# First pass's chunk steps placed ahead for all chunks, and the last block's first tiles prepared beside the last pairs

## The reference, cut to what matters

```python
xn = _layernorm(x, axis=-1)
x = x + _L0_gnn_ref(xn, ..., edge_index, edge_type_8) + _L0_mix_ref(xn[None], ...)[0]      # attention over edges, 8 heads
x = x + _L0_ffn_ref(_layernorm(x, axis=-1)[None], ...)[0]                                  # shared MLP + 2 of 8 experts
xn = _layernorm(x, axis=-1)
x = x + _L1_gnn_ref(xn, edge_index, ...) + _L1_mix_ref(xn[None], ...)[0]                   # GCN, then GAT
x = x + _L1_ffn_ref(_layernorm(x, axis=-1)[None], ...)[0]                                  # MLP of the better half of the nodes
```

## Time and profile before

| what | us |
|---|---|
| median of 3 runs | 2853.38 (2851.15 to 2854.49) |
| profiled execution | 2854.25 |
| its span | 2852.4 |

### The profile page before, as it was taken

One profiled execution on the slowest core, in us unless ns is written; L12 is line 12 of the kernel. 1 busy time (PEld: TensorE's weight loads), 2 busy tenths in 40 slices (PEclk: granted clock), 3 DMA queues, 4 the chain that ended last, 5 costly groups with the idle time before them and its releaser, 6 DMA issues. The chain is left out here.

```text
span 2852.4 us, 42642 instructions
## 1 busy us (share of the span) xinstructions
PE 2291.0 (80%) x11329; PEld 1711.2 (60%) x11329; DVE 1313.4 (46%) x3497; ACT 1076.8 (38%) x2885; POOL 1377.5 (48%) x1407
## 2 busy tenths in 40 slices
PE   6899847767677988999997787877754888875798
PEld 5455535445455877888886465554543777764577
DVE  6553456766676130111114232242248666655851
ACT  3323544545441211333333443265420665542221
POOL 0122477777730051212211677767767777775300
PEclk9999867888788899999998898888775999998899
DMA  3466544444411025777774433344557444443201
GB/s 98 153 219 220 181 110 122 119 120 118 119 50 41 10 95 152 196 221 205 210 211 130 141 106 106 106 122 124 162 147 236 125 132 134 131 123 116 95 12 33
DMA packets 249527, 374.45 MB, mean 131 GB/s; under 512 B 66472, under 2 KB 186740, under 8 KB 249322
## 3 DMA queue, kind: packets, MB, share of 16 engines
q0 software_dynamic: 70000, 179.80, 22.8%
q1 hardware_dynamic: 132740, 140.88, 16.1%
q10 hardware_dynamic: 46582, 51.38, 5.5%
HBM read 298.68 MB, written 73.27 MB: 130 GB/s over the span
## 5 line engine op out<-in xcount | busy, mean ns | idle before, releaser
L2724 POOL DMA_INDIRECT cm_rows<-rows,e_bsrc x392 | 373.3, 952 | 179.0 <-issue 101.2
L1181 POOL DMA_INDIRECT store<-rows,e_bsrc x392 | 377.3, 963 | 119.5 <-issue 107.3
L1459 POOL DMA_INDIRECT at_rows<-values,e_brow x362 | 344.8, 953 | 115.1 <-issue 90.5
L2861 PE MATMUL cm_part<-cm_rows,cm_one 128*128 x880 | 268.0, 447 | 89.8 <-SPq L2737 62.8
L1539 PE MATMUL at_part<-at_msg,store 128*128 128x265 f32 x880 | 269.1, 448 | 86.8 <-DVE at_msg L1695 42.7
L1206 PE MATMUL banks<-ag_msg,ag_one 128*128 128x258 f32 x880 | 228.0, 397 | 70.3 <-issue 45.7
L2861 PEld LDWEIGHTS cm_part<-cm_rows,cm_one 128*128 128x128 f32 x880 | 181.7, 220 | 158.7 <-issue 134.9
L1539 PEld LDWEIGHTS at_part<-at_msg,store 128*128 128x128 f32 x880 | 175.8, 218 | 156.7 <-DVE at_msg L1695 66.7
L2161 POOL DMA_INDIRECT x_sum<-x_y,x_target x56 | 87.1, 1555 | 340.7 <-DVE x_y L2274 333.3
L3077 DVE TENSOR_TENSOR store<-store,cm_part 128x256 f32 x220 | 92.2, 419 | 339.1 <-PE cm_part L2861 311.1
L1206 PEld LDWEIGHTS banks<-ag_msg,ag_one 128*128 128x128 f32 x880 | 165.4, 195 | 117.2 <-issue 57.3
(11 more groups left out here) (685 smaller groups left out, 3920.2 us busy)
## 6 DMA issues: line engine op xcount, KB each, us to landing
x_w<-in_L_ffn_W1p SPq DMA_DIRECT2D x32, 1024.0 KB, 5.2
x_w<-in_L_ffn_W2p SPq DMA_DIRECT2D x32, 1024.0 KB, 5.5
values<-at_rows ACTq DMA_DIRECT2D x25, 1088.0 KB, 6.0
p_brow<-local_row SPq DMA_DIRECT2D x44, 320.0 KB, 4.0
xn_acc<-low_row SPq DMA_DIRECT2D x28, 448.0 KB
expert_in<-store POOLq DMA_DIRECT2D x7, 1040.0 KB, 8.1
at_rows<-values,e_brow POOLq DMA_INDIRECT x392, 2.8
cm_rows<-rows,e_bsrc POOLq DMA_INDIRECT x392, 2.7
```

What stands on the lines that cost most here:

```text
L1181: pool.indirect_dma_start(rows[:, b % slots, k, :], None, table, bass.IndirectOffsetOnAxis(index[:, k, b:b + 1], 0)).then_inc(gathered[b % ...
L1459: pool.indirect_dma_start(rows[:, b % RING, k, :], None, table, bass.IndirectOffsetOnAxis(e.block_row[:, k, b:b + 1], 0)).then_inc(gathere ...
L2724: pool.indirect_dma_start(rows[:, b % SLOTS, k, :], None, table, bass.IndirectOffsetOnAxis(e.block_src[:, k, b:b + 1], 0)).then_inc(gather ...
L2861: last = pe.matmul(part[:, n % deep, :], one[:, n // U % 2, k, u, :], rows[:, bass.ds(at[u] % SLOTS, 1), k, :].squeeze(1), start=(k == 0), ...
```

## The change

In `attend`, PE's six steps of every chunk after the first stand at the pairs lo − 10, − 7, − 6, − 5, − 4 and − 2, and ACT's slope, exponent and fade at lo − 9, lo − 3 and lo, as they did for the last chunk alone; DVE's steps stay. FREE becomes 25: ACT fetches the scores of 25 pairs ahead and SP frees a block 25 blocks after it. In `convolve_and_mix`, AIMED has 23 as well, so four more tiles are scattered there and two are left for `score2`. In `aggregate`, a new class `FirstTiles` loads the table rows and x rows of tiles 0 to 4 after block 98's arrival, and DVE does the degree operations, join, divide, residual and statistics for these five tiles between pairs 202 and 214. In `finish`, group 0 is no longer fetched or prepared: DVE copies the statistics, goes on with variance, root and slots of group 0, then does the degree operations for all tiles, then `prepare(1)`. The loads are put in another order, and w1 and b1 have a semaphore of their own.

```diff
...
                 sp.sem_inc(ready, 1)
+                if b == NB // 2:
+                    firsts.fetch(sp)
...
+                firsts.work(dve, n, summed)
...
+    def fetch(self, sp):
+        sp.wait_ge(*self.gate)
+        sp.dma_start(self.h, self.table[0:U * P].rearrange("(t p) d -> p t d", p=P)).then_inc(self.loaded, 16)
+        sp.dma_start(self.x, self.x_rows[:, 0:U, :]).then_inc(self.loaded, 16)
...
+    def work(self, dve, n, summed):
+        at = n - (NB + U + 1)
+        if at == 0:
+            dve.wait_ge(summed, NB + U - 1)
+            self.ahead(dve)
+            self.link(dve, dve.tensor_scalar(self.some, self.degree[:, 0:U], 1.0, None, ALU.is_lt))
...
+            dve.wait_ge(self.loaded, 32)
+        if at in range(1, 2 * U + 4):
+            self.ahead(dve)
+        for u in range(U):
+            if at == 2 * u + 1:
+                self.link(dve, dve.scalar_tensor_tensor(out=self.h[:, u, :], in0=self.h[:, u, :], scalar=self.own[:, u:u + 1], in1=self.acc[:, u, 0:D],
+                                                        op0=ALU.mult, op1=ALU.add))
+            if at == 2 * u + 2:
+                self.link(dve, dve.scalar_tensor_tensor(out=self.h[:, u, :], in0=self.h[:, u, :], scalar=self.inv[:, u:u + 1], in1=self.bias[:],
+                                                        op0=ALU.mult, op1=ALU.add))
+            if at == 2 * u + 3:
+                self.link(dve, dve.scalar_tensor_tensor(out=self.x[:, u, :], in0=self.h[:, u, :], scalar=0.0, in1=self.x[:, u, :],
+                                                        op0=ALU.max, op1=ALU.add))
+            if at == 2 * u + 4:
+                self.link(dve, dve.bn_stats(self.st[:, u, :], self.x[:, u, :]))
...
-RING, FREE = 28, CH + LEAD
+RING, FREE = 28, CH + LEAD + 3
...
-    pe_steps, act_steps = ({n: step for n, step in step_of.items() if step[1] != last_at} for _ in range(2))
-    pe_steps.update({last_at + d: (len(CHUNKS) - 1, *CHUNKS[-1], i) for i, d in enumerate((-10, -7, -6, -5, -4, -2))})
-    act_steps.update({last_at + d: (len(CHUNKS) - 1, *CHUNKS[-1], i) for i, d in ((0, -9), (3, -3), (6, 0))})
+    pe_steps, act_steps = ({n: step for n, step in step_of.items() if step[0] == 0} for _ in range(2))
+    for pc, (lo, m) in enumerate(CHUNKS[1:], 1):
+        pe_steps.update({lo + d: (pc, lo, m, i) for i, d in enumerate((-10, -7, -6, -5, -4, -2))})
+        act_steps.update({lo + d: (pc, lo, m, i) for i, d in ((0, -9), (3, -3), (6, 0))})
+    soon = [min(G, n + 1 + (FREE if n >= 0 else CH + LEAD)) for n in range(-LEAD, G)]
...
-            for n in range(FREE - LEAD):
+            for n in range(CH):
                 fetch(n)
+            have = CH
             for n in range(-LEAD, G):
                 if n == hurry:
-                    for late in range(n + FREE, G):
+                    for late in range(have, G):
                         fetch(late)
-                if n > hurry and n in act_steps:
+                    have = G
+                if n > 0 and n in act_steps:
                     softmax(*act_steps[n])
                 if n >= 0 and n % U == 0 and n + U < G:
                     hots(n // U + 1)
-                if n < hurry:
-                    fetch(n + FREE)
+                for late in range(have, soon[n + LEAD]):
+                    fetch(late)
+                have = max(have, soon[n + LEAD])
                 if n > 0 and n % 8 == 0 and n // 8 + 1 < NT:
                     take(n // 8 + 1)
-                if n <= hurry and n in act_steps:
+                if n <= 0 and n in act_steps:
...
-AIMED = (8, 14, 19)
+AIMED = (8, 14, 19, 23)
 EARLY = AIMED[-1]
...
-            fetch(0)
-            bring(0)
+            sp.dma_start(w1[:], mlp_in[0].rearrange("(k p) f -> p k f", p=P)).then_inc(up_loaded, 16)
+            sp.dma_start(b1[:], columns_of(mlp_in[1]), allow_slow_non_contiguous=True).then_inc(up_loaded, 16)
+            fetch(1)
+            bring(1)
+            sp.dma_start(w2[:], mlp_in[2].rearrange("(k p) f -> p k f", p=P)).then_inc(mlp_loaded, 16)
+            sp.dma_start(b2[:], row_of(mlp_in[3]).broadcast_to([P, D])).then_inc(mlp_loaded, 16)
             sp.dma_start(wr[:], router[0].rearrange("d e -> e d").broadcast_to([P, D])).then_inc(router_loaded, 16)
             sp.dma_start(br[:], row_of(router[1]).broadcast_to([P, 1])).then_inc(router_loaded, 16)
-            fetch(1)
-            bring(1)
-            sp.dma_start(w1[:], mlp_in[0].rearrange("(k p) f -> p k f", p=P)).then_inc(mlp_loaded, 16)
-            sp.dma_start(b1[:], columns_of(mlp_in[1]), allow_slow_non_contiguous=True).then_inc(mlp_loaded, 16)
-            sp.dma_start(w2[:], mlp_in[2].rearrange("(k p) f -> p k f", p=P)).then_inc(mlp_loaded, 16)
-            sp.dma_start(b2[:], row_of(mlp_in[3]).broadcast_to([P, D])).then_inc(mlp_loaded, 16)
             for g in range(2, NT // U):
                 bring(g)
             for g in range(2, NT // U):
-                sp.wait_ge(grown, (g - 1) * U)
+                if g > 2:
+                    sp.wait_ge(grown, (g - 2) * U)
                 fetch(g)
...
-                pool.tensor_tensor(x[:, t, :], x[:, t, :], slot[:, t % (2 * U), :], ALU.add).then_inc(blended, 1)
+                pool.tensor_tensor(x[:, t, :], first.x[:, t, :] if t < U else x[:, t, :], slot[:, t % (2 * U), :], ALU.add).then_inc(blended, 1)
...
-            pe.wait_ge(mlp_loaded, 64)
+            pe.wait_ge(up_loaded, 32)
...
+                if j == 0:
+                    pe.wait_ge(mlp_loaded, 32)
...
-                dve.wait_ge(fetched[g % 2], 16 * (g // 2 + 1))
+                dve.wait_ge(fetched[g % 2], 16 * ((g + 1) // 2))
...
-                dve.wait_ge(stats, (g + 1) * U)
+                dve.wait_ge(stats, g * U)
+                normalise(g, x)
+
+            def normalise(g, x):
+                of = [(u, g * U + u) for u in range(U)]
                 mo.variance(dve, link, g * U, U, varied)
...
+            link(dve.tensor_copy(mo.st[:, 0:U, :], first.st))
+            normalise(0, first.x)
             link(dve.tensor_scalar(some[:], degree[:], 1.0, None, ALU.is_lt))
...
-            prepare(0)
             prepare(1)
...
```

More of the change, by code:

```diff
@@ L1153, with aggregate @@
 LAG = 5
-def aggregate(nc, tag, c, e, index, table, heads, weights, factors, acc, ring, banks, gate, ride):
+def aggregate(nc, tag, c, e, index, table, heads, weights, factors, acc, ring, banks, gate, ride, firsts):
     width = table.shape[1]
@@ L1164, in aggregate @@
     with Mem(nc) as m, stage(nc, "cleared", "ready", "freed", "whole", "apart", "hot", "weighted", "multiplied", "summed",
-                             *(f"gathered{b}" for b in range(slots)), *(ride.NAMES if ride else ())) as (
-            block, cleared, ready, freed, whole, apart, hot, weighted, multiplied, summed, *others):
+                             *firsts.NAMES, *(f"gathered{b}" for b in range(slots)), *(ride.NAMES if ride else ())) as (
+            block, cleared, ready, freed, whole, apart, hot, weighted, multiplied, summed, first_in, first_chain, *others):
+        firsts.place((first_in, first_chain))
         gathered = others[0:slots]
@@ L1270, in _, with __init__, place, link @@
                     add_up(n - 2, tiles[(n - 2) % U])
+                firsts.work(dve, n, summed)
             add_up(G - 2, tiles[U - 2])
             add_up(G - 1, tiles[U - 1])
+class FirstTiles:
+    NAMES = ("first_in", "first_chain")
+    def __init__(self, space, acc, degree, bias, table, x_rows, gate):
+        self.acc, self.degree, self.bias, self.table, self.x_rows, self.gate = acc, degree, bias, table, x_rows, gate
+        size = U * D
+        self.h, self.x = (space[:, n * size:(n + 1) * size].rearrange("p (t d) -> p t d", d=D) for n in range(2))
+        self.st = space[:, 2 * size:2 * size + 6 * U].rearrange("p (t q) -> p t q", q=6)
+        at = 2 * size + 6 * U
+        self.some, self.n, self.inv_n, self.own, self.den, self.inv = (space[:, at + n * U:at + (n + 1) * U] for n in range(6))
+    def place(self, names):
+        self.loaded, self.chain = names
+        self.done = 0
+    def fetch(self, sp):
+        sp.wait_ge(*self.gate)
+        sp.dma_start(self.h, self.table[0:U * P].rearrange("(t p) d -> p t d", p=P)).then_inc(self.loaded, 16)
+        sp.dma_start(self.x, self.x_rows[:, 0:U, :]).then_inc(self.loaded, 16)
+    def link(self, dve, ins):
+        self.done += 1
+        ins.then_inc(self.chain, 1)
+    def ahead(self, dve):
+        dve.wait_ge(self.chain, self.done)
+    def work(self, dve, n, summed):
[5 more added lines that the diff above has]
+            self.ahead(dve)
+            self.link(dve, dve.tensor_scalar(self.n, self.degree[:, 0:U], 1.0, None, ALU.max))
+            self.ahead(dve)
+            self.link(dve, dve.reciprocal(self.inv_n, self.n))
+            self.ahead(dve)
+            self.link(dve, dve.tensor_tensor(self.own, self.acc[:, 0:U, D + 1], self.inv_n, ALU.mult))
+            self.ahead(dve)
```

(29 more changed lines are left out.)

15 lines of the change are left out of this document (8 added, 7 removed).

## The result

The changed kernel takes 2908.11 us (median of 4 runs, 2902.83 to 2911.22) against 2853.79 (the kernel before, with a fourth run): 1.019 times the time before, 95% interval 1.0175 to 1.0204. It is 54 us slower where 2838 was forecast, and outside the range of 2830 to 2848. In the profiled executions, of which that of the changed kernel is its fastest run (2902.83), the span went from 2852.4 to 2901.0 us.

| part | before, us | after, us | difference | forecast |
|---|---|---|---|---|
| before the first edge pass | 359.4 | 361.4 | +2.0 | 0 |
| first edge pass (attend) | 502.3 | 560.3 | +58.0 | −3 |
| to the first gather of convolve_and_mix | 721.3 | 721.7 | +0.4 | 0 |
| its gathers | 497.5 | 492.8 | −4.7 | 0 |
| its last gather to the second edge pass's first | 41.9 | 42.3 | +0.4 | −3.3 |

A forecast was written before the change was run, and what follows sets the result against it. Gathers were taken to bound both edge passes, and DVE's work the finish. Finish −9.4, first tiles 0, scatters −3.3 and first edge pass −3 sum to −15.7 us on the median of 2853.38: 2838 us, range 2830 to 2848.

The forecast's parts named there:

- First edge pass: attend: only the lag behind the last gather can shrink; taken at −3 us, bounds −6.5 and +2.
- the price of PE's early steps: First edge pass: PE waits in order for just-landed scores, with up to four pairs' products queued behind; bounded at +2 us.
- the stage runs at the pace of the gathers: First edge pass: a chunk is 14.25 blocks at 2.51 us of gathers, 35.8 us, so POOL never really waits.
- 29 to 31 us of consumer work from one turn to the next: First edge pass: consumer work after chunk 12's turn at 789 to 791.5, putting the last turn at 818.5 to 822.5 us.
- The lag of 6.5 us: End of first edge pass: the most the last chunk's turn could gain, 823.2 − 816.7 us.
- DVE's stalls before L1628: First edge pass: DVE's 86.6 us waiting for ACT's slope, to go mostly with hardly any time won.
- The slow rival: First edge pass: gathers run out of slots through later freeing and PE's in-order wait; 2865 us, chance 0.10.
- the sign that the prediction named for being wrong: First edge pass: gathers showing waits on SyncE above 0.3 us would mean the prediction is wrong.
- Finish: Finish: first fetch and four rounds of operations leave DVE's path, group 1 begins 8.45 us after the start; −9.4 us.
- First tiles: End of second edge pass: DVE's added operations covered by its slack beside the last pairs; 0 us, up to +3.
- Scatters: convolve_and_mix to score2: four scatters moved save 5.2 us, their stage ends 1.9 later; −3.3 us (−4.0 to +1.0).
- its first rival: Only the finish gains: scatters' landing of 5.6 to 7.8 us eats their term, first pass unchanged; 2844 us, chance 0.21.

The follow-up runs named there:

- half_after: The changed kernel with one of the two gathers of each block left out in the first edge pass: first pass 567.2 us, 2911.11 us in all.
- half_turn: The changed kernel with PE's steps 1 to 5 back at lo − 5 to lo − 1 and one of each block's two first-pass gathers left out: 2819.57 us.
- half_before: The kernel before with one of the two gathers of each block left out in the first edge pass: first pass 502.4 us, 2856.91 us in all.
- turn_early: The changed kernel with PE's steps 1 to 5 back at lo − 5 to lo − 1, only step 0 early at lo − 10: 2838.62 us.
- free22: The changed kernel with SyncE freeing block b − 22 as before, ACT still looking 25 ahead: 2908.00 us.
- dve_early: The changed kernel with DVE's steps 0, 2, 3 and 5 of a chunk two pairs sooner as well: 2848.80 us.

## Why the prediction was wrong, point by point

**First edge pass, taken at −3 us, measured +58.** The step that failed is the price of PE's early steps, bounded at +2. The bound named the right place ("the products of up to four pairs are queued behind that wait"), but only for step 0's wait for scores. Steps 1, 2, 3 and 5 were not set against DVE's list, where the steps that feed them had stayed, and so were put at nothing. It is there that 94.8 us of waits arose: 7.4 us a chunk for the consumers alone (half_after against half_turn), 4.0 us a chunk times 11 beyond the time before, plus 12.9 to the last one.

The bound looked safe because "the stage runs at the pace of the gathers". The arithmetic was right (35.8 us a chunk is 14.25 blocks at 2.51 us), but the same 35.8 us was what the consumers took, as half_before shows. Equal numbers were taken for a cause, and the consumers were taken to have time to lose. For the early step 0 the reasoning held: turn_early's first pass is 2.0 us shorter than before, where −3 was taken.

"29 to 31 us of consumer work from one turn to the next" failed too: no row of before stands beside it, and a middle chunk takes 39.8 us with these offsets. Four pairs are 4/16 of 35.8 us, 9 us, and not "some 6 us". The lag of 6.5 us that could be won at the end grew: the last turn came 883.28 − (859.0 + 2.8) = 21.5 us after the last rows, where before it was 7.2.

**DVE's stalls before L1628** The earlier trace rows did go, as was foreseen (86.6 to 11.6 us), and no time came of it. DVE now stands in its waits for PE instead.

**The slow rival** had the right sign and the right stage, and the sign that the prediction named for being wrong, waits for SyncE above 0.3 us, came. Its mechanism was wrong: free22 frees the slots by the old rule and gains nothing, and half_after, whose gathers need half the time, loses no less.

**Finish, −9.4 us: right, with two errors that cancel.** The steps can be read one by one (after; timeline of DVE, the stage starts at 2687.5):

```profile
2687.55 0.23 DVE L3471 COPY fi_st<-first 128x30 f32<-128x30 f32 x1 [4.21 <-PEq L60]
...
2691.03 2.93 DVE L3468 TENSOR_SCALAR fi_slot<-first,fi_mean,fi_rs 128x256 f32<-128x256 f32 x5
```

The slots come 3.5 us after the start, as worked out. Group 1 began at 2697.02, 9.5 us after the start and not 8.45: the first two degree operations took 0.70 and 0.65 us beside POOL's adds, where the term had 0.23 and 0.18. The rows of group 1 did come close to being late, as feared. In the chain that ended last it is their fetch that leads to group 1, and not DVE's work as the prediction's sign had it:

```profile
2688.47 8.45 DMA fi_h<-rows
2697.02 2.07 DVE fi_h L3434 x5
```

8.45 us from an issue 1 us after the stage's start: landed 9.4 us after it where 7.9 was worked out, 0.1 us before use. So the gain at group 1's start is 8.4 us. Most of the other 1.0 is in its join, the row that starts there: 2.07 us where before took 2.92, since POOL's adds are over by then. Beside POOL's adds it is now the degree operations that are slower.

**First tiles, 0 us: right, with a cover that it didn't name.** It takes 11.5 us from the last gather to the finish in both profiles, with all 28 operations done beside the last pairs. By the instruction records DVE's last addition ends 6.7 us after the last gather's start before and 7.3 after, while a DRAIN of POOL holds the stage until 10.2 us in both. So 0.6 us of DVE's delay was left at the end and lay under that DRAIN.

**Scatters, −3.3 us: wrong, measured +0.4.** "The store that ends the stage" was right. The failed step is the term for how much later the stage ends with the moved scatters, 1.9 us, worked out from a landing of about 2.8 us. They landed sooner, in 2.1 us, but POOL's DRAIN of 5.2 us comes after the landing, so that the stage goes on 9.3 us after the last scatter; and POOL's waits for targets were not in the sum. The gain at score2's front did come: four scatters fewer, 5.4 us. The prediction's sentence on the Trainium skill ("DMA: Bandwidth & Descriptors", section "Anatomy of one DMA — SWDGE (gpsimd) path"), that a semaphore is raised only after a write receipt and that device memory is the slowest target, stood beside its first rival, a landing nearer 5.6 us. The traces don't agree with that estimate: these scatters, which write there, landed in 2.1 us, sooner than the gathers' 2.8.

The 4.7 us that convolve_and_mix's gathers were shorter are not the change's doing as far as the runs tell: they took 490.3 to 497.5 us across these kernels, and what sets that wasn't tried.

## What to carry to other kernels

Before calling a resource the bound because its rate matches, look for a second one with the same rate. The waits of the engine that stands between the two (here SP) show it in the trace, and halving the work of the suspect (here one of two gathers) shows it in one run. Do the same for the end of a stage: what a later last instruction costs depends on how close the second-latest engine is. When a step is moved in one in-order engine's list, find the place of the step that feeds it in the other engine's list: a step placed ahead of its feeder stops both, and a step that is moved together with its feeder costs little (dve_early). Step 0 moved alone cost nothing here, although PE stood 56.9 us before it (turn_early). A gain hidden under an equal limit is still there for the next change: half_turn shows 24 us that only faster gathers would bring out.

## What was not expected of the hardware

An indirect scatter of 128 rows of 8 bytes to device memory landed 2.1 us after its issue, but a stage whose last work on POOL it was went on 9.3 us after it, in all nine profiles with 23 scatters: POOL's list has a DRAIN of 5.2 us there. At the end of the second edge pass such a DRAIN ends 10.2 us after the start of the last gather, which landed after 3.8 (before). What the DRAIN waits for isn't shown. In the first pass of the kernel before, halving the gathers' number left the time as it was, 502.3 and 502.4 us (one run): the full set of gathers, running all the time beside the consumers, did not slow them by any amount that shows.
